# Eight experts' gather and scatter through two DRAM tables of normed row and running sum, on one Trainium2 core

## What is computed

```python
def _L0_ffn_ref(x, Wr, W1, b1, W2, b2):      # x: the normed rows, N = 4 * 3138, D = 128, E = 8, F = 512, C = 1024
    x_flat = x.reshape(N, Dd)
    logits = x_flat @ Wr
    probs = jax.nn.softmax(logits, axis=0)
    vals, idx = jax.lax.top_k(probs.T, C)
    selected = x_flat[idx]
    h = jax.nn.gelu(jnp.einsum('ecd,edf->ecf', selected, W1) + b1[:, None, :], approximate=False)
    out_e = jnp.einsum('ecf,efd->ecd', h, W2) + b2[:, None, :]
    weighted = vals[..., None] * out_e
    output = jnp.zeros_like(x_flat).at[idx.reshape(-1)].add(weighted.reshape(-1, Dd))
...
    h = h + _L0_ffn_ref(_layernorm(h, axis=-1), L0_ffn_Wr, L0_ffn_W1, L0_ffn_b1, L0_ffn_W2, L0_ffn_b2)
    h = h + _L1_attn_ref(_layernorm(h, axis=-1), L1_attn_w_qkv, L1_attn_w_proj, L1_attn_b_proj)
    h = h + _L1_ffn_ref(_layernorm(h, axis=-1), L1_ffn_ln_scale, ...)
```

## Time and profile before

| | us |
|---|---|
| median of 3 runs | 2762.41 |
| lowest and highest of them | 2756.27, 2762.47 |
| the profiled execution, time | 2761.4 |
| its span in the profile | 2759.4 |

### The profile page before, as it was taken

One profiled execution on the slowest core, in us unless ns is written; L12 is line 12 of the kernel. 1 busy time (PEld: TensorE's weight loads), 2 busy tenths in 40 slices (PEclk: granted clock), 3 DMA queues, 4 the chain that ended last, 5 costly groups with the idle time before them and its releaser, 6 DMA issues. The chain is left out here.

```text
span 2759.4 us, 26470 instructions
## 1 busy us (share of the span) xinstructions
PE 2294.0 (83%) x6899; PEld 1098.8 (40%) x6899; DVE 2382.7 (86%) x3555; ACT 1616.4 (59%) x3023; POOL 2068.2 (75%) x1108
## 2 busy tenths in 40 slices
PE   5999999999999999999984148717888888888888
PEld 2444444444444444444432024304444444444444
DVE  3999999999999999999996832226999999999996
ACT  4777777767777777777662124424545555555544
POOL 2889899898898898988992048766777777777772
PEclk8999999999999999999996569857999999999999
DMA  2243333333433333333333013311111111011100
GB/s 75 94 124 99 106 115 105 114 111 93 128 98 108 118 106 110 116 93 115 108 96 98 0 35 73 47 25 31 31 29 30 29 28 31 28 31 31 31 24 23
DMA packets 180609, 199.44 MB, mean 72 GB/s; under 512 B 40062, under 2 KB 170988, under 8 KB 180332
## 3 DMA queue, kind: packets, MB, share of 16 engines
q1 hardware_dynamic: 169196, 189.35, 22.5%
q0 software_dynamic: 11264, 8.40, 2.3%
HBM read 164.44 MB, written 33.25 MB: 72 GB/s over the span
## 5 line engine op out<-in xcount | busy, mean ns | idle before, releaser
L915 POOL TENSOR_TENSOR a_hc<-a_h,a_cs 128x896 f32<-128x896 f32 (+1 forms) x448 | 859.6, 1938 | 55.4 <-DVE a_h L778 54.9
L362 PE MATMUL a_y_bank<-a_hc,a_ident 128*128 128x448 f32 (+1 forms) x1792 | 741.4, 544 | 20.3 <-DVE a_yz L798 19.7
L553 ACT ACTIVATE a_da<-a_dt,a_neg_a 128x448 f32<-128x448 f32 (+1 forms) x896 | 551.8, 631 | 295.6 <-DVE a_h L778 290.6
L778 DVE TENSOR_TENSOR_SCAN a_h<-a_da,a_h,a_dbx 128x448 f32<-128x448 f32 x528 | 583.3, 1135 | 9.5 <-ACT a_da L553 4.4
L362 PEld LDWEIGHTS a_y_bank<-a_hc,a_ident 128*128 128x128 f32 x1792 | 331.6, 190 | 325.2 <-issue 273.0
L2183 POOL TENSOR_TENSOR c_prod<-c_prob,c_qkv 128x1024 f32<-128x1024 f32 x100 | 279.3, 2820 | 189.3 <-DVE c_prob L2053 189.3
L1777 PE MATMUL c_p_E<-c_w_ex,c_hid 128*128 128x512 f32 x800 | 375.4, 599 | 38.3 <-DVE c_sc L2029 36.3
L762 DVE TENSOR_TENSOR a_dbx<-a_dtx,a_b_bank 128x896 f32<-128x896 f32 (+1 forms) x308 | 327.8, 1064 | 15.7 <-PE a_b_bank L355 15.5
L2174 POOL TENSOR_TENSOR c_prod<-c_qkv 128x1024 f32<-128x1024 f32 x100 | 232.7, 2353 | 58.1 <-ACT c_qkv L1845 58.1
L903 POOL TENSOR_TENSOR a_dbp<-a_dtx,a_bs 128x896 f32<-128x896 f32 (+1 forms) x140 | 270.9, 1935 | 0.0
L778 DVE TENSOR_TENSOR_SCAN a_h<-a_da,a_h,a_dbp 128x448 f32<-128x448 f32 x240 | 263.4, 1130 | 0.0
(11 more groups left out here) (306 smaller groups left out, 3744.1 us busy)
## 6 DMA issues: line engine op xcount, KB each, us to landing
a_cs<-c_rows SPq DMA_DIRECT2D x96, 896.0 KB, 5.3
a_bs<-c_rows SPq DMA_DIRECT2D x24, 1120.0 KB, 5.7
a_cs<-c_rows SPq DMA_DIRECT2D x16, 900.0 KB, 4.4
c_x<-h_rows SPq DMA_DIRECT2D x100, 64.0 KB, 2.3
heads<-c_ot SPq DMA_DIRECT2D x25, 256.0 KB, 2.0
c_dealt<-heads SPq DMA_DIRECT2D x200, 32.0 KB, 1.9
rolled<-c_res SPq DMA_DIRECT2D x25, 256.0 KB, 2.4
h_rows<-a_th SPq DMA_DIRECT2D x24, 224.0 KB
```

Source lines behind the costliest of these rows:

```text
L362: pe.matmul(y_bank[:, d, 0:g.w], ident[:], hc[:, (g.i * NS + n) % HC_RING, d, 0:g.w], start=(n == 0), stop=(n == NS - 1)).then_inc(s_sum, 1)
L553: act.activation(da[:, k % DA_RING, 0:g.w], dt[g.slot][:, d, 0:g.w], ACT.Exp, scale=neg_a[:, d * NS + n:d * NS + n + 1]).then_inc(s_da, 1)
L778: dve.tensor_tensor_scan(h[:, n, d, 0:g.w], da[:, (g.i * 2 * NS + k) % DA_RING, 0:g.w], x, state, ALU.mult, ALU.add).then_inc(s_scan, 1)
L915: pool.tensor_tensor(hc[:, (q.i * NS + n) % HC_RING, :, 0:q.w], h[:, n, :, 0:q.w], cs[:, n % C_RING, 0:q.w].unsqueeze(1).to_broadcast([P, ...
```

## The change

The two tables of 512-byte rows become two tables `rows0` and `rows1` whose rows hold 256 values: the normed row in the first half and a running sum in the second. Stage A writes `rows0` (normed row and the row itself). While the lists are made, SP copies the normed halves into `rows1` with four transfers of 3208 rows and fills its sum halves with zeros from SBUF with eight transfers; these twelve are issued ahead of the experts' weights.

Even experts work on `rows0`, odd ones on `rows1`. A gather now brings 1024 bytes a row, normed row and sum. DVE adds share times output to the sum in place, with one `scalar_tensor_tensor` a tile (eight an expert) instead of one multiplication a half, and POOL writes the whole 1024-byte rows back with a plain indirect transfer, no longer an accumulating one. So gather e has to wait until all scatters of e-2 have landed, and gather 1 until `rows1` is complete; the scatters wait for no other scatter. The gathers now run one expert ahead at most, in another order on POOL.

PE takes the two halves in turn: transposes of half 0, first product of half 0, then transposes and first product of half 1.

Stage C loads both sums, eight transfers a group instead of four, and a new call `merge` on POOL adds the second tile to the first, behind `add_experts(0)`; DVE's `stats_of` waits for it instead of for the load. The load of group L also waits for the merge of group L-2.

```diff
-        h_rows = dram("h_rows", [ROWS, D])
-        n_rows = dram("n_rows", [ROWS, D])
+        tables = [dram(f"rows{k}", [ROWS, 2 * D]) for k in range(2)]
+        n_rows, h_rows = tables[0][:, 0:D], tables[0][:, D:2 * D]
...
@@ phase_b, sync: behind the loads of constants, ahead of the weights
+        for b in range(BATCH):
+            span = slice(b * ROWS // BATCH, (b + 1) * ROWS // BATCH)
+            sp.dma_start(tables[1][span, 0:D], tables[0][span, 0:D]).then_inc(s_second, 16)
+        sp.wait_ge(s_fill, 2)
+        for top in range(0, ROWS, P * NZERO):
+            n = min(P * NZERO, ROWS - top)
+            per = NZERO if n == P * NZERO else n // 32
+            sp.dma_start(tables[1][top:top + n, D:2 * D].rearrange("(p k) d -> p k d", k=per),
+                         zeros[0:n // per, 0:per * D].bitcast(F32).rearrange("p (k d) -> p k d", k=per)
+                         ).then_inc(s_second, 16)
...
@@ phase_b, vector
-            need(dve, s_scatter, 16 * TILES * (e - 1))
             for h in range(2):
                 dve.wait_ge(s_turned, 2 * e + h + 1)
-                dve.tensor_tensor(og[s][:, h * HT:(h + 1) * HT, :], p_t[h][:].rearrange("p (i d) -> p i d", i=HT),
-                                  share[s][:, h * HT:(h + 1) * HT].unsqueeze(2).to_broadcast([P, HT, D]), ALU.mult
-                                  ).then_inc(s_og, 1)
+                for i in range(HT):
+                    t = h * HT + i
+                    total = xg[e % XG][:, t, D:2 * D]
+                    last = dve.scalar_tensor_tensor(out=total, in0=p_t[h][:, i * P:(i + 1) * P], scalar=share[s][:, t:t + 1],
+                                                    in1=total, op0=ALU.mult, op1=ALU.add)
+                last.then_inc(s_og, 1)
...
@@ phase_b, tensor
                 mm.then_inc(s_tr, 1)
-            pe.wait_ge(s_w[s], 32 * (e // 2 + 1))
-            for h in range(2):
+                if h == 0:
+                    pe.wait_ge(s_w[s], 32 * (e // 2 + 1))
                 pe.wait_ge(s_xt, 2 * e + h + 1)
                 for f in range(FT):
...
@@ phase_b, gpsimd
         def gather(e):
+            if e == 1:
+                pool.wait_ge(s_second, 16 * SECOND)
+            if e >= 2:
+                pool.wait_ge(s_scatter, 16 * TILES * (e - 1))
...
-                pool.indirect_dma_start(xg[e % XG][:, i, :], None, n_rows[:, :],
+                pool.indirect_dma_start(xg[e % XG][:, i, :], None, tables[e % 2][:, :],
...
         def scatter(e):
-
-            need(pool, s_scatter, e * 16 * TILES)
...
-                pool.indirect_dma_start(h_rows[:, :], bass.IndirectOffsetOnAxis(ap=index[:, i, e:e + 1], axis=0),
-                                        og[e % 2][:, i, :], None, compute_op=ALU.add).then_inc(s_scatter, 16)
+                pool.indirect_dma_start(tables[e % 2][:, :], bass.IndirectOffsetOnAxis(ap=index[:, i, e:e + 1], axis=0),
+                                        xg[e % XG][:, i, :], None).then_inc(s_scatter, 16)
-        for e in range(XG - 1):
+        for e in range(2):
             gather(e)
         for e in range(E0):
-            if e + XG - 1 < E0:
-                gather(e + XG - 1)
             scatter(e)
+            if e + 2 < E0:
+                gather(e + 2)
...
@@ phase_c, sync: load
-                    rows = h_rows[L * GW + SHIFT:(L + 1) * GW + SHIFT, :].rearrange("(w n) d -> n w d", n=WIN)
-                    for j in range(GT):
-                        sp.dma_start(x[L % 3][:, j, :],
-                                     rows[j * WIN // GT:(j + 1) * WIN // GT]).then_inc(s_x[L % 3], 16)
+                    need(sp, s_merged, L - 1)
+                    for table, tile, done in ((tables[0], x[L % 3], s_x[L % 3]), (tables[1], x2[L % 2], s_x2[L % 2])):
+                        rows = table[L * GW + SHIFT:(L + 1) * GW + SHIFT, D:2 * D].rearrange("(w n) d -> n w d", n=WIN)
+                        for j in range(GT):
+                            sp.dma_start(tile[:, j, :], rows[j * WIN // GT:(j + 1) * WIN // GT]).then_inc(done, 16)
...
@@ phase_c, vector: stats_of
-                    dve.wait_ge(s_x[L % 3], (L // 3 + 1) * 16 * GT)
+                    dve.wait_ge(s_merged, L + 1)
...
@@ phase_c, gpsimd
+            def merge():
+                if L is not None:
+                    pool.wait_ge(s_x[L % 3], (L // 3 + 1) * 16 * GT)
+                    pool.wait_ge(s_x2[L % 2], (L // 2 + 1) * 16 * GT)
+                    pool.tensor_tensor(x[L % 3][:], x[L % 3][:], x2[L % 2][:], ALU.add).then_inc(s_merged, 1)
...
             score_products(2)
             add_experts(0)
+            merge()
             score_products(3)
```

## The result

| | before | after |
|---|---|---|
| median of 4 runs each, us | 2762.22 | 2783.76 |
| lowest and highest | 2756.27, 2762.47 | 2779.28, 2784.99 |
| ratio, 95% interval | | 1.0080, 1.0063 to 1.0098 |
| span of the profiled execution | 2759.4 | 2782.4 |
| first gather to first load of stage C | 211.94 | 208.16 |

The time lies inside the predicted range (2752 to 2790) and 15 us above the predicted 2769. The forecast had said "the same" by 0.3%; this is slower by 0.8%. Stage C came as forecast, +28.1 us against +28.9. The experts gave back 3.8 us instead of 20.9 between first gather and first load. So the question was where 17 us of gain went. The changed kernel's program alone does not explain it: the same program, measured again later, took 2767.85 us beside 2755.41 (ratio 1.0037, 1.0023 to 1.0050).

What follows compares the result with a forecast made beforehand. The prediction took POOL's indirect transfers to bound the experts and DVE to bound stage C's full turns. Stage C's 28.9 us minus the experts' 20.9 gave +8.0 on 2761.4, hence 2769 us, range 2752 to 2790.

Steps and rivals of the forecast that it cites:

- Second table: Filling during the routing: copies and zeros all in by 1590 us at the latest, hidden, zero cost.
- Price of a scatter: POOL in the experts: a plain scatter costs the gather's 0.952 us, against 1.554 for an accumulating one.
- Eight DVE instructions: Experts' scaling on DVE: the eight small instructions add 0.1 us a half, with no wait for POOL.
- First scatter: Start of the experts: half 0's earlier product gains 2.1 us, so the first scatter starts at 1642.5.
- Period and end: POOL's expert loop: period 21.84 us, 3.7 less; first load of stage C at 1800.9, 20.9 us earlier.
- PE fits ... 19.0: Experts: PE's 17.46 us plus some 1.5 for exposed transposes and copy, 19.0, fits POOL's period.
- Stage C: Second sum's cost: +3.9 us at the first group, +3.0 in filling turns, +22.0 in twenty full turns; 28.9.
- Merge absorbed: Rival, stage C: POOL adds earlier or DVE recovers the delay, only 3.9 + 3 remain; 2747 us, chance 0.10.
- Late output of the first expert goes away: Rival, expert 0: some 5 us unexplained before its scaling vanish if the third gather group caused them; 2764, chance 0.15.
- Second table late: Rival, filling: copying beyond 104 us delays weights and gather 1; 2815 at 94 ns a row, chance 0.12.
- scatters as dear as accumulating ones: Rival, experts: plain scatters cost what accumulating ones do; 2803 us, chance 0.08.
- DVE held by POOL: Rival, experts: each of eight DVE instructions waits up to 1.25 us for POOL's transfers; 2777, chance 0.05.

Runs made afterwards that it cites:

- h_after: The changed kernel, not altered, measured again in the last comparison: 2767.85 us, ratio 1.0037.
- h_before: The kernel before, not altered, measured again in the last comparison: 2755.86 us, ratio 1.0000.
- e_bhalf: The kernel before with one edit, PE working half by half: 2757.56 us, ratio 0.9998.
- e_front: The changed kernel with the merge moved to the front of POOL's turn, ahead of score_products(0): 2759.6 us, ratio 1.0007.
- f_swap: The changed kernel with the merge in front and the two tables exchanged between even and odd experts: 2742.08 us, ratio 0.9958.
- f_ring: The changed kernel with the merge in front and 16 spare gathers ahead of the first: 2763.37 us, ratio 1.0037.
- g_swap_late: The changed kernel with only the two tables exchanged, the merge left in its place: 2768.29 us, ratio 1.0054.
- g_swap_ring: The changed kernel with the merge in front, tables exchanged and 16 spare gathers ahead: 2762.38 us, ratio 1.0027.
- g_front: e_front again, byte for byte, in a later comparison: 2742.06 us, ratio 0.9956.
- e_peold: The changed kernel with PE's old order, transposes of both halves, then first product of both: 2784.0 us, ratio 1.0092.

## Why the prediction was right or wrong, point by point

**Second table: right.** In by 1563, against 1590 at the latest. While SP issues the copies, the DMA share is 0.57, some 9 of 16 engines, and it is the same from 1505 to 1519 us, where nothing but the copies runs; over the stretch of the zeros it is 0.89. The first share is near the Trainium skill's rule ("DMA: Bandwidth & Descriptors", Why a DMA increments its semaphore by 16 and not by 1), by which 3208 rows go over 8 engines, which would read 0.50; which engines worked no trace here tells. What refuted the rival was the row's price: 170 GB/s x 30 us are 9960 rows of 512 bytes, and 0.57 x 30 x 16 / 9960 = 27 ns a row, the low end of 27 to 94.

**Price of a scatter: right.** 0.971 against an assumed 0.952.

**Eight DVE instructions: mis-sized.** Four take 1.13 us, not 0.69 + 0.1; 0.44 instead of 0.1 a half. No instruction waited for POOL: a group of four took 1.12 or 1.13 us in every half. The second group delayed the copy of the next expert's half 0 by 0.75 us, and PE then waited 1.53 us before its product, where before it was 0.56. The loop hid that.

**First scatter: forecast 4 us too late.** 1642.5 against 1637.96 on record and 1638.25 in h_after. The 5 us that I had left in the sum as unexplained came again neither in the changed kernel nor in h_before.

**Period and end: right in h_after, wrong on record.** Forecast 21.84, measured 21.9. Forecast for the last scatter group and the first load: 1789.3 and 1800.9; measured 1787.17 and 1798.58. The one step outside is the first, 23.55 us, with a landing of 3.52. On record they were 1805.28 and 1816.64. The step of the prediction that failed is "PE fits ... 19.0". The 19.0 itself was right (outputs are 19.24 us apart where PE waits neither for a late completion nor for gathered rows), but it left only 2.8 us of reserve a period. Late completions of 3 to 5 us, with the low clock behind them, made three steps 9 us longer, to 28 and 29, and put 18.2 us on the stretch (208.16 against 189.93 in h_after). The kernel before lost less: its medians differ by 7 us between the first and the last comparison, the changed kernel's by 16, those of the version with the merge in front by 17.5 on one chip. It has 8 us of reserve, 17.5 under 25.5, but that this hid late completions is not shown: its traces of the first two comparisons, before and e_bhalf, have only one of about 3 us or more each, at expert 0, where POOL has to wait for the output anyway. Why it had one and the changed kernel four stays open. I had seen one such place, at expert 0, and treated it as a chance of gain only. The rival that ought to have stood there is the slower one: more such places, in a loop in which PE has less reserve.

**Stage C: right in sum, two terms off.** On record +28.1 up to the last statistics, and the tail the same: 4.3 at the first load (forecast 3.9), 6.5 in four filling turns (3.0: the turns take 17.18, 25.44, 26.92 and 35.32 instead of 14.82, 24.20, 26.88 and 32.43), 17.3 in twenty full turns (22.0). The turn is 35.97 us as forecast (36.1, 34.9 + 1.07), but before, some turns were longer by themselves (one 37.49), and in the changed kernel, where DVE is idle for 0.97 us a turn, all twenty take 35.95 to 35.99. In h_after against h_before the whole is 34.3: 28.7 from first to last statistics, 4.4 at the first load, 1.2 in the tail.

**The rivals.** Merge absorbed: no, but e_front shows that it can be, by its place. Late output of the first expert goes away: it did (1636.56 where 1643.53 stood), and so did it in h_before, so it was no gain of the change. Second table late, scatters as dear as accumulating ones, DVE held by POOL: all refuted by the rows above.

**The numbers.** 2769 against 2767.85 in the last comparison and 2783.76 on record. That the time on record lies inside the range is luck: the upper end, 2790, stood there for rivals that did not come. Part of the agreement in the last comparison is chance too: beside h_before the experts' gain is 18.0, not 20.9, stage C's cost is 34.3, not 28.9, and the base lay 7 us lower. The difference measured is 12.4 us, or 10.2 by the ratio, where I gave 8 and "the same, close to its edge": it lay a little beyond the edge of 8.3 us, and the interval of the ratio reaches to either side of it.

## What to carry to other kernels

When one engine sets the pace by a few us, look for the next one's reserve, not only for its mean: the change took POOL's period from 25.5 to 21.9 and left PE 2.8 us, and steps of PE of 28 us then showed in the time, about 6 us each. (An estimate: under 25.5 they would have shown by 2 to 3 each.) An addition on an engine with idle time is free at one place of its turn and costs nearly its full length (1.1 of 1.27 us) at another: put it in front of the wait that hangs on a third engine. And before edits of a kernel are compared over several comparisons, run one of them again unedited; f_swap and f_ring looked for the cause of the standstills with no unedited version beside them, and in the comparison of g_swap_late and g_swap_ring the unedited version had none to remove.

The version with the merge in front (g_front, ratio 0.9956) beats both kernels when completions come in time, and equals the kernel before (e_front, 1.0007) when they do not.

## What was unexpected of the hardware

- TensorE's completions arrived 3 to 5 us late at one to four places of the experts' part, with the records of its matmuls (their ends are modelled) in time. It happened in the six traces of the first two comparisons and in none of the eight later ones, with the same chip in one comparison of each kind, and with one kernel, byte for byte, in both. It was seen only in the experts' part, where POOL writes indirect transfers; in stages A and C no wait of these traces was released by "remote". Its cause stays open. It comes with either order of PE, without a second table and without a third gather group beside it (e_peold, before, after), and it can stay away with the same chip, kernel, tables and transfer numbers (g_front). What sets the places within a comparison that has it is not shown.
- A plain indirect scatter of 128 rows takes POOL 0.97 us, an accumulating one 1.55, and the DMA share while a group is written falls from 0.38 to 0.14 with rows of 512 bytes, though the plain group moves more bytes a us (52 GB/s against 33). In the kernel before that is worth 41 us.
- Four `scalar_tensor_tensor` of 128 columns take 1.13 us where one multiplication of 512 took 0.69.
